# Linear attention, second batch: statistics of the first FFN block's rows two steps earlier, normalisation one step ahead, T3/T4 halves one step later

## The reference

```python
x = x + linear_attention(layernorm(x), Wq, bq, Wk, bk, Wv, bv, ...)
#   per chunk: attn = (q @ k.T) * beta * decay;  y = attn @ v + (q @ state) * chunk_decay
#              state = state * total_decay + v.T @ (k * beta * decay_to_end)
x = x + ffn(layernorm(x))      # silu(x @ Wg) * (x @ Wu) @ Wd, weights (codes - 128) * scale
x = x + attention(layernorm(x), W_q, W_k, W_v, W_o)
x = x + ffn(layernorm(x))
```

## Time and profile before

| what | value |
|---|---|
| median of 3 runs | 1017.73 us (1017.63 to 1019.08) |
| the profiled execution, its own time | 1019.8 us |
| its span in the profile | 1018.1 us |
| PE busy | 970.5 us, 95% of the span, 4818 matmuls |
| DVE, ACT, POOL busy | 568.9, 406.7, 427.2 us (56, 40, 42%) |
| mean granted PE clock | 0.992 |
| chain that ended last | PE 79%, DVE 9%, POOL 4%, issue 3%, ACT 3%, DMA 1% |

### The profile page before, as it was taken

The page is one execution under the profiler, slowest core; times in us unless marked ns, Lnnn a source line. Parts: engine busy times, 40 slices in busy tenths (PEclk is TensorE's granted clock), DMA queues, the critical chain, the costliest instruction groups (busy, mean ns, idle before and its releaser), DMA issues.

```text
span 1018.1 us, 12993 instructions
## 1 busy us (share of the span) xinstructions
PE 970.5 (95%) x4818; PEld 549.3 (54%) x4818; DVE 568.9 (56%) x1092; ACT 406.7 (40%) x790; POOL 427.2 (42%) x440
## 2 busy tenths in 40 slices
PE   7999999987999999998989999999998999999997
PEld 4888888876744444443444445545454444444443
DVE  7566747567467666654453334623365576666542
ACT  4332323335477634663222211322133566346630
POOL 5554435458437665555310000000024466655553
PEclk9999999999999999999999999999999999999999
DMA  9200200013030000000000000000000000010001
GB/s 330 97 1 1 114 1 1 1 42 125 11 114 1 1 1 1 1 1 1 1 1 1 1 1 1 1 1 1 1 1 1 1 1 1 32 52 1 1 22 62
DMA packets 12302, 26.05 MB, mean 26 GB/s; under 512 B 1744, under 2 KB 1744, under 8 KB 12240
## 3 DMA queue, kind: packets, MB, share of 16 engines
q1 hardware_dynamic: 12240, 25.22, 6.8%
HBM read 21.02 MB, written 4.19 MB: 25 GB/s over the span
## 4 chain that ended last, share of the span: by engine, by line
PE 79%; DVE 9%; POOL 4%; issue 3%; ACT 3%; DMA 1%; SPq 0%; POOLq 0%; DVEq 0%; ACTq 0%
PE psum L1745 51%; PE psum L1970 13%; PE psum L1972 12%; PE psum L2097 2%; PE psum L1778 1%; PE psum L1767 1%; POOL hid L756 1%; DMA wqk_raw<-wk 1%; DVE xres L1370 1%; DVE xq L1225 1%; DVE state L1357 1%; DVE xn L1202 1%; POOL xrstd L610 1%; DVE wv_lo L1256 1%; DVE ln_bn L1192 1%
## 5 line engine op out<-in xcount | busy, mean ns | idle before, releaser
L760 POOL TENSOR_TENSOR hid<-hid,hid_hi 128x512 f32<-128x512 f32 x88 | 102.0, 1159 | 93.6 <-DVE hid_hi L1499 93.6
L1970 PE MATMUL psum<-xf,w_gu 128*128 128x512 f16 x352 | 133.8, 380 | 0.0
L1970 PE MATMUL psum<-xf,w_s 128*128 128x512 f16 x264 | 100.0, 379 | 1.9 <-DVE up L1472 1.3
L1972 PE MATMUL psum<-xf,w_gu 128*128 128x512 f16 x264 | 100.1, 379 | 0.0
L789 POOL TENSOR_TENSOR yt<-yt,sd_rows 128x512 f32<-128x512 f32 x32 | 51.7, 1617 | 61.1 <-DVE yt L1549 61.1
L604 POOL TENSOR_TENSOR ln_rstd<-ln_var,minus_half 128x1 f32<-128x1 f32 x28 | 16.5, 594 | 140.1 <-DVE ln_var L1168 140.1
L610 POOL TENSOR_TENSOR xrstd<-xvar,minus_half 128x1 f32<-128x1 f32 x32 | 19.1, 600 | 124.6 <-DVE xvar L1196 124.6
L1012 ACT ACTIVATE hid_lo<-hid 128x512 f16<-128x512 f32 x88 | 54.9, 624 | 33.5 <-POOL hid L760 33.5
L756 POOL TENSOR_TENSOR hid<-up,gate 128x512 f32<-128x512 f32 x44 | 55.9, 1271 | 27.0 <-ACT gate L1007 27.0
L1972 PE MATMUL psum<-xq,w_s 128*128 128x512 f16 x176 | 66.7, 379 | 0.0
L1970 PEld LDWEIGHTS psum<-xf,w_gu 128*128 128x128 f16 x352 | 34.3, 97 | 54.1 <-ACT acc L997 15.5
(11 more groups left out here) (275 smaller groups left out, 2411.9 us busy)
## 6 DMA issues: line engine op xcount, KB each, us to landing
out<-xres SPq DMA_DIRECT2D x16, 256.0 KB, 2.0
xres<-x SPq DMA_DIRECT2D x3, 1024.0 KB, 13.5
codes_gu<-gateT SPq DMA_DIRECT2D x1, 2816.0 KB, 16.7
codes_gu<-upT SPq DMA_DIRECT2D x1, 2816.0 KB, 10.7
codes_da<-downT SPq DMA_DIRECT2D x1, 1536.0 KB, 6.9
codes_db<-downT SPq DMA_DIRECT2D x1, 1280.0 KB, 9.9
xres<-x SPq DMA_DIRECT2D x4, 256.0 KB, 3.0
wqk_raw<-wk SPq DMA_DIRECT2D x1, 1024.0 KB, 7.6
```

The source lines that it names most:

```text
L760: nc.gpsimd.tensor_tensor(hid[:, :], hid[:, :], hid_part(hid_hi, j, half), ALU.subtract).then_inc(rest_done, 1)
L1970: nc.tensor.matmul(bank(use[0]), w, x_operand(piece, k, False), start=start and k == 0, stop=False, skip_group_check=not start)
L1972: last = nc.tensor.matmul(bank(use[0]), w, x_operand(piece, k, True), start=False, stop=k == 1, skip_group_check=not start)
```

## The change

PE's list is the same, instruction for instruction, and so is SP's. On DVE, ACT and POOL the same instructions stand in another order. On DVE, statistics of all eight tiles are made in steps (0,2) and (0,3) (one tile ahead of `attn_out`, one behind it, two after `y_out`); pair i + 1 is normalised behind `x_second` of pair i; `x_34_low` of pair i moves from the end of its step into the next step, between `k_out` and `attn_out`; and the four low halves of `wkT` move from behind the last `y_out` to between `attn_out` and `y_out` of step (1,3). On ACT, `x_34_high` moves from the end of its step to behind `kT_out` and `decay_out` of the next one, and the `wqT` high halves of steps (1,1) and (1,2) stand behind it there. On POOL, the powers of pairs 1 to 3 are made in step (0,3), and the `wqT` low halves stand ahead of `scale_k`.

```diff
@@ constants
-X_STATS = ((0, 2), (0, 3), (1, 0), (1, 1))
+X_STATS = {(0, 2): ((0,), (1,), (2, 3)), (0, 3): ((4,), (5,), (6, 7))}
@@ POOL, step (s, c) of linear attention
                             weight_k(s, c)
+                        if b == 1 and (s, c) == (0, 3):
+                            x_rstd(0, 2, 3)
+                        if b == 1 and (s, c) in ((1, 1), (1, 2)):
+                            for k in (0, 1) if c == 1 else (2, 3):
+                                pool.wait_ge(wqT_hi_done, k + 1)
+                                nc.gpsimd.tensor_tensor(cols(qk_lo, k), cols(qk_raw, k), cols(qk_hi, k).bitcast(F32),
+                                                        ALU.subtract).then_inc(wq_split, 1)
                         if c < 3:
                             scale_k(s, c + 1)
@@
                             x_12_low(0, X_STEPS.index((s, c)))
-                        if b == 1 and (s, c) in X_STATS:
-                            x_rstd(0, X_STATS.index((s, c)))
-                        if b == 1 and (s, c) in ((1, 1), (1, 2)):
...
+                        if b == 1 and (s, c) == (0, 2):
+                            x_rstd(0, 0, 1)
+                        if b == 1 and (s, c) == (0, 3):
+                            x_rstd(0, 4, 5, 6, 7)
@@ ACT, step (s, c)
                         decay_out(s, c)
+                        if b == 1 and s == 1:
+                            x_34_high(0, c)
+                        if b == 1 and (s, c) in ((1, 1), (1, 2)):
...
                         if c < 3:
                             norms(s, c + 1)
@@
-                        if b == 1 and (s, c) in X_STEPS:
-                            x_34_high(0, X_STEPS.index((s, c)))
-                        if b == 1 and (s, c) in ((1, 1), (1, 2)):
...
@@ DVE, step (s, c)
+                        rows = X_STATS.get((s, c), ((), (), ())) if b == 1 else ((), (), ())
...
-                        if pair is not None:
-                            x_normalise(0, pair)
                         if c < 3:
                             k_out(s, c + 1)
...
+                        for r in rows[0]:
+                            x_stats(0, r)
+                        if b == 1 and s == 1 and c < 3:
+                            x_34_low(0, c)
                         attn_out(s, c)
+                        for r in rows[1]:
+                            x_stats(0, r)
+                        if b == 1 and (s, c) == (1, 3):
+                            x_34_low(0, 3)
+                            for k in range(KT):
+                                dve.wait_ge(wk_hi_done, k + 1)
+                                nc.vector.tensor_tensor(cols(qk_lo, KT + k), cols(qk_raw, KT + k),
+                                                        cols(qk_hi, KT + k).bitcast(F32),
+                                                        ALU.subtract).then_inc(wk_split, 1)
...
                             x_second(0, pair)
+                            if pair < 3:
+                                x_normalise(0, pair + 1)
                         if (s, c) != (1, 3):
                             state_out(s, c)
                         y_out(s, c)
+                        for r in rows[2]:
+                            x_stats(0, r)
+                        if b == 1 and (s, c) == (0, 2):
+                            x_normalise(0, 0)
...
-                        if pair is not None:
-                            x_34_low(0, pair)
-                        if b == 1 and (s, c) in X_STATS:
...
@@ DVE, stage "mid"
-            for k in range(KT):
-                dve.wait_ge(wk_hi_done, k + 1)
...
```

More of the change, by code:

```diff
@@ L605, in rstd, with x_rstd @@
                                         minus_half[:, 0:1], ALU.pow).then_inc(ln_rstd_done, 1)
-            def x_rstd(blk, i):
-                for l in (2 * i, 2 * i + 1):
+            def x_rstd(blk, *rows):
+                for l in rows:
                     pool.wait_ge(ln_var_done, ln_n("X", blk, l) + 1)
@@ L737, in _ @@
                             x_12_low(0, X_STEPS.index((s, c)))
-                        if b == 1 and (s, c) in X_STATS:
-                            x_rstd(0, X_STATS.index((s, c)))
-                        if b == 1 and (s, c) in ((1, 1), (1, 2)):
-                            for k in (0, 1) if c == 1 else (2, 3):
-                                pool.wait_ge(wqT_hi_done, k + 1)
-                                nc.gpsimd.tensor_tensor(cols(qk_lo, k), cols(qk_raw, k), cols(qk_hi, k).bitcast(F32),
-                                                        ALU.subtract).then_inc(wq_split, 1)
+                        if b == 1 and (s, c) == (0, 2):
+                            x_rstd(0, 0, 1)
+                        if b == 1 and (s, c) == (0, 3):
+                            x_rstd(0, 4, 5, 6, 7)
             def ffn(phase, b):
@@ L779, in ffn @@
                     if b == 0 and j in (2, 4, 6, 8):
-                        x_rstd(blk + 1, (j - 2) // 2)
+                        x_rstd(blk + 1, j - 2, j - 1)
                 for t in range(BT):
@@ L813, in _ @@
             for i in range(4):
-                x_rstd(2, i)
+                x_rstd(2, 2 * i, 2 * i + 1)
                 if i > 0:
@@ L950, in _ @@
                         decay_out(s, c)
+                        if b == 1 and s == 1:
+                            x_34_high(0, c)
+                        if b == 1 and (s, c) in ((1, 1), (1, 2)):
+                            act.wait_ge(wqT_in, 16)
+                            for k in (0, 1) if c == 1 else (2, 3):
+                                nc.scalar.activation(cols(qk_hi, k), cols(qk_raw, k), ACT.Copy).then_inc(wqT_hi_done, 1)
                         if c < 3:
@@ L969, in _ @@
                             head(1)
-                        if b == 1 and (s, c) in X_STEPS:
-                            x_34_high(0, X_STEPS.index((s, c)))
-                        if b == 1 and (s, c) in ((1, 1), (1, 2)):
-                            act.wait_ge(wqT_in, 16)
-                            for k in (0, 1) if c == 1 else (2, 3):
-                                nc.scalar.activation(cols(qk_hi, k), cols(qk_raw, k), ACT.Copy).then_inc(wqT_hi_done, 1)
             def ffn(phase, b, extra):
@@ L1405, in _ @@
                             split_lo("A", b, l)
-                        attn_out(s, c)
+                        if b == 1 and (s, c) == (0, 2):
+                            Use(dve, "A", 0).read_out((7, 7))
+                            dve.wait_ge(gu_ready, 8)
+                        for r in rows[0]:
+                            x_stats(0, r)
+                        if b == 1 and s == 1 and c < 3:
+                            x_34_low(0, c)
+                        attn_out(s, c)
+                        for r in rows[1]:
[7 more added lines that the diff above has]
+                                                        ALU.subtract).then_inc(wk_split, 1)
                         if c < 3:
@@ L1444, in _ @@
                                     stats("A", b, l)
-                        if pair is not None:
-                            x_34_low(0, pair)
-                        if b == 1 and (s, c) in X_STATS:
-                            i = X_STATS.index((s, c))
-                            if i == 0:
-                                Use(dve, "A", 0).read_out((7, 7))
-                                dve.wait_ge(gu_ready, 8)
-                            x_stats(0, 2 * i)
-                            x_stats(0, 2 * i + 1)
             def ffn(phase, b, extra):
@@ L1579, in weight_sums @@
                 nc.vector.tensor_tensor(two(w_s, 4), two(w_gu, 2), two(w_s, 0), ALU.subtract).then_inc(ws_ready, 1)
-            for k in range(KT):
-                dve.wait_ge(wk_hi_done, k + 1)
-                nc.vector.tensor_tensor(cols(qk_lo, KT + k), cols(qk_raw, KT + k), cols(qk_hi, KT + k).bitcast(F32),
-                                        ALU.subtract).then_inc(wk_split, 1)
             Use(dve, "A", 1).read_out((7, 7))
```

## The result

The changed kernel takes 1009.71 us, the median of 4 runs (1007.64 to 1010.81), beside 1018.40 us for the kernel before on the same chip (1017.63 to 1019.97): a ratio of 0.9909, with a 95% interval of 0.9890 to 0.9927. It is faster by 8.7 us. The forecast was 1002.0 us, 7.7 us less, and the range ended at 1006.0.

The account below looks back on a forecast made before the run. PE was taken as the bound, busy 970.5 of 1018.1 us. Gains of 8.99 + 4.49 + 3.59 = 17.07 us less new waits of 0.5, 0.5 and 0.4 gave 15.7, so 1002.0 us against 1017.73; range 999.8 to 1006.0.

Parts of the forecast that it names:

- point 5: New waits of PE from step (1,1) to "mid" once the old ones go: 0.5, 0.5 and 0.4 us taken off.
- (a): Steps (1,2) and (1,3): POOL's 12.63 us cycle exceeds PE's 11.14, so PE waits for `steps_hi`; 0.5 us, at worst 1.8.
- (c): Before "mid": `x_34_low` and the first low half stand behind `attnT` on DVE; PE waits 0.4 us, between 0 and 1.
- Points 2 and 3: Steps (1,0) to (1,3): earlier `xn` and later `x_34_low` gain 8.99 us; `kT` ahead of `x_34_high` and `qk_hi` gains 4.49.
- Point 1: Steps (0,2) and (0,3): moving the statistics of eight tiles there costs PE nothing, 0 us.
- 5(b): Step (1,3): `attnT` stands behind `state` and `y_out` of (1,2) on DVE; PE waits 0.5 us, between 0 and 1.
- Point 4: Start of "mid": `wkT` low halves ahead of `y_out` remove a 1.94 us wait and 1.65 of slow products, 3.59 us.
- 5(d): Weight loads before "mid": `wo` is all there by 243.3 us; at most 1 us on ACT, nothing on PE.
- rival B: The loads become late once PE's waits no longer give them time: 6 us lost, 1008 us; chance 5%.
- A: POOL becomes the bound of steps (1,1) to (1,3), with the clock falling behind the longer wait: 1004.9 us; chance 13%.
- C: The gain is given back downstream, in "mid" or at the FFN's start: no change, 1017.7 us; chance 4%.
- D: PE's clock falls and stays down from step (1,1) to the end of "mid": slower, 1039 us; chance 3%.

Follow-up runs that it names:

- xn_head2: The changed kernel with each pair normalised at the head of its own step again, second run of that kernel: 1009.16 us, ratio 0.9897.
- wq_back: The changed kernel with POOL's `wqT` low halves back at the end of their step, as before the change: 1011.04 us, ratio 0.9919.
- wq_dve: The changed kernel with the `wqT` low halves of steps (1,1) and (1,2) made by DVE behind `attn_out`, not by POOL: 1005.55 us, ratio 0.9853.
- wvt_wait: The changed kernel with POOL's `wvT` and `wo` halves started only when DVE is done with the `wkT` low halves: 1007.36 us, ratio 0.9882.
- both2: Second run of the changed kernel with `wqT` low halves on DVE and POOL's `wvT` held behind DVE's `wkT` low halves: 1004.99 us, ratio 0.9859.
- both: The changed kernel with `wqT` low halves on DVE and POOL's `wvT` held behind DVE's `wkT` low halves: 1004.89 us, ratio 0.9850.

## Why the prediction was wrong

It named each wait that would go, and they went. It missed by 7.7 us: 3.8 up to the mark, 1.7 behind it, 2.1 in the base, and 0.1 of rounding. Its own test fails as well: from the first product of "mid" to the end of the span it wanted 760.2 - 1.65 = 758.5 us, and there are 1007.9 - 245.37 = 762.5. The mechanism was right, and two terms of point 5 were mis-sized: (a) went below what the row of POOL's cycle gave, and (c) costed instructions at lengths that they do not keep beside POOL's work.

- **Points 2 and 3, what goes: right.** No turn waits for `xn`, none for `kT` or the copy, and the clock is 1.00 from 216 to 250 us. Within point 2, the credit for normalising ahead was misplaced (`xn_head2`: 0).
- **Point 5(a), POOL: wrong by 1.7 us.** The step that failed is "I take 0.5 for both", with its reason that "12.63 is an upper end". The new waits for `kn` and `steps_hi` from 227 us on come to 0.74 + 0.53 + 0.58 + 0.34 = 2.2 us. POOL's cycle, from the end of one `steps_hi` to the end of the next, is 226.97 + 1.22 - 213.49 - 1.49 = 13.2 us and then 240.45 - 228.19 = 12.3: together 25.5, where twice 12.63 is 25.3. The row was a fair mean, not an upper end, and PE's 11.14 could not be had. The rest is that POOL began at 214.98 us and not at 214.6, as its `steps_hi` took 1.49 us and not 1.04. (The reckoned worst case of 1.8 counts the 0.2 twice; 1.6 is the whole lateness at 239.8.) The sentence that the `qk_lo` ahead of `scale_k` do not add to the cycle stood up: in `wq_back`, with them behind, POOL is done with these steps at 245.66 us and not at 244.08.
- **Point 1, the statistics: wrong by 0.4 us.** It was put at 0. The wait for `kn` at 179 us is 0.60 where it was 0.16. By the rows, the statistics of step (0,2) put DVE's `steps_lo` from 176.88 to 177.18 us, beside POOL's `kscale`, which took 0.64 us instead of 0.20. No run moved the statistics back.
- **5(b), `attnT`: 0.5 forecast, none came.** PE was late enough from (a). In `wq_dve`, without that lateness, 0.47 for `state` and 0.16 for `attnT` stand there, so the term was right in size.
- **Point 4 with 5(c), the start of "mid": wrong by 2.0 us.** There are 2.4 us of waits instead of 0.4. The term took 0.7 us for the T3/T4 low half, which stands ahead of the first `wkT` half; beside POOL's last low half of T1 and T2 it took 1.61, and PE waited 1.07 (0.77 and 0.22 in `wq_dve`). And it took a quarter of 2.69 us for each `wkT` half. It had moved them to where POOL makes `wvT_lo` and `wo_lo`, and the four took 4.67: two more waits, 0.60 and 0.73, which `wvt_wait` takes away.
- **5(d), the loads: right.** PE had no wait for them in the change. `both2`'s 0.83 us for a `wo` half is the kind of rival B, at a seventh of its size.
- **The sum.** 17.07 less 2.2, 0.4 and 2.4 is 12.1 us, and the mark moved 11.9, or 11.5 without the offset of 0.4. The closeness is in part luck, since the waits that went and those that came both cost more than their printed numbers. The repaired kernel `both` bears out the 17.07 in size: its mark moved 16.7, with 1.3 us of small new waits left in it. The forecast's stated upper end of about 1003.5 has only (a) at its worst; with (b) and (c) at theirs too it would be 1004.5.
- **"Everything behind moves up with it": wrong by 1.7 us**, one more fall of the clock, behind waits that were there before.
- **The forecast's base: 2.1 us.** This is no mechanism but where single executions fell. I had taken off the 2.1 us by which the profiled execution stood above its median. The profile of the change is at its own median (1009.61 and 1009.71). Beside the experiments the kernel before had medians of 1019.5 to 1021.6 us: the three runs shown were at its low end.

Of the rivals, A was nearest, with 1004.9: POOL did become the bound, and its waits of 2.2 us were above A's 1.8, but the clock did not fall behind them. C and D did not come as written. Against the prediction's own choice stood the rule that it had cited from the Trainium skill (Advanced Engine Details and Errata, VectorE Performance Modes), that a port of VectorE is shared with GpSimd and that its two-port instructions and GpSimd's block each other. `wvt_wait` agrees in size: four instructions of 2.48 us in all took 4.67 beside POOL. That the `wkT` halves are two-port instructions is not shown by any run.

## What to carry to other kernels

When a wait of the bounding engine is removed, ask for each instruction that you move what the other engine does in the stretch where it lands, and cost it at the stretched duration, here 1.9 times for the `wkT` halves and 2.4 for the T3/T4 ones, when both DVE and POOL work from SBUF there. An engine whose cycle is longer than the bounding engine's falls behind it step by step: here POOL's 12.7 us a step met PE's 11.1, reordering its list only moved the wait (3.17 us in `wq_back`), and taking 2.5 to 3.0 us of work a step off it removed it (`wq_dve`). And the worth of an edit read from its wait is an upper end until what stands behind that wait is shown to be early: here the same edit brought 1.3 us and 5.1.

## What was not expected of the hardware

- Which DVE instructions were stretched: only such as read and write SBUF, and not all of these. `xn` took 0.99 us a pair in a quiet stretch and 1.72 beside POOL's scaling, T3/T4 low halves 0.68 to 1.61, the `wkT` halves 2.48 to 4.67. Those that read PSUM kept their time beside the same POOL work: `attnT` at 221.20 took 0.68 us while POOL made `qk_lo`. Nor is it always DVE that loses: the T3/T4 low half at 232.37 us took its 0.68, and POOL's `kw` beside it 1.44 instead of 1.05. The two rows of `xn`, from the timeline of DVE in the change:

```profile
192.97 0.99 DVE L1207 TENSOR_SCALAR xn<-xres,xmv,xrstd 128x512 f32<-128x512 f32 x2
...
225.57 1.72 DVE L1207 TENSOR_SCALAR xn<-xres,xmv,xrstd 128x512 f32<-128x512 f32 x2
```

- PE's clock: behind the same waits in the same list it fell in some profiles and not in others, of one kernel too, at 1.7 us each time, and one to three such falls make up the differences in the time behind the mark. A forecast for this kernel finer than some 2 us can't be had from one profile.
